# First-batch query parts of both attentions copied inside SBUF by two queues, in place of a store to DRAM and a load back

## What is computed

```python
q = (query @ Wq.T).reshape(B, q_len, H, dk).transpose(0, 2, 1, 3)
k = (key @ Wk.T).reshape(B, k_len, H, dk).transpose(0, 2, 1, 3)
v = (value @ Wv.T).reshape(B, k_len, H, dk).transpose(0, 2, 1, 3)
scores = jnp.einsum('bhqd,bhkd->bhqk', q, k) / jnp.sqrt(jnp.float32(dk))
attn = jax.nn.softmax(scores, axis=-1)
out = jnp.einsum('bhqk,bhkd->bhqd', attn, v)
x = x + out.transpose(0, 2, 1, 3).reshape(B, q_len, D) @ Wout.T + b_out
```

## Time and profile before

| | us |
|---|---|
| median of 3 runs | 1268.6 |
| profiled execution, first to last instruction | 1262.1 |
| PE busy in all | 1123.7 (89%) |
| attention 0, first to last matmul | 4.6 to about 226 |
| attention 1, first to last matmul | 470.3 to about 698 |

### The profile page before, as it was taken

How to read it: one execution, slowest core, us unless ns; L and a number is a source line. 1 busy time by engine, 2 the same in 40 slices (tenths; PEclk the granted TensorE clock), 3 DMA queues, 4 the chain that set the end, 5 groups by cost and what they waited for, 6 DMA issues and landing times. The chain is left out here.

```text
span 1262.1 us, 25941 instructions
## 1 busy us (share of the span) xinstructions
PE 1123.7 (89%) x8539; PEld 974.6 (77%) x8539; DVE 690.8 (55%) x1558; ACT 595.9 (47%) x1211; POOL 360.7 (29%) x502
## 2 busy tenths in 40 slices
PE   5999998739999984888998679999999999999997
PEld 4788786329888873555665379999999999999996
DVE  4755666652222226676767655555556555555556
ACT  3566666313222222776787334444445444444432
POOL 6566650112222205776630145000000000000261
PEclk8899999859999996999999879999999999999999
DMA  7774461548999957568471221223232232232132
GB/s 182 175 180 120 129 179 37 193 159 292 332 330 325 314 207 163 111 136 146 89 125 24 100 89 59 79 63 112 72 103 76 87 109 87 86 100 73 50 97 80
DMA packets 88137, 172.56 MB, mean 137 GB/s; under 512 B 11251, under 2 KB 59949, under 8 KB 81792
## 3 DMA queue, kind: packets, MB, share of 16 engines
q1 hardware_dynamic: 71712, 136.15, 39.0%
q0 software_dynamic: 9584, 29.32, 7.9%
q10 hardware_dynamic: 6768, 6.16, 1.4%
HBM read 133.11 MB, written 39.20 MB: 137 GB/s over the span
## 5 line engine op out<-in xcount | busy, mean ns | idle before, releaser
L2136 PE MATMUL e_ps<-xT_e,wp_e 128*128 128x384 f32 (+1 forms) x1344 | 245.2, 331 | 4.0 <-DVE wp_e L2010 4.0
L2136 PEld LDWEIGHTS e_ps<-xT_e,wp_e 128*128 128x128 f32 x1344 | 221.7, 188 | 5.4 <-issue 4.1
L639 DVE TENSOR_REDUCE att_ps<-att_ps 128x2 f32<-128x512 f32 (+1 forms) x224 | 155.3, 697 | 103.5 <-PE att_ps L986 63.2
L1968 ACT ACTIVATE act_a_e<-e_ps 128x256 f32<-128x256 f32 (+2 forms) x176 | 77.8, 442 | 159.9 <-PE e_ps L2136 150.9
L2066 DVE TENSOR_TENSOR hid_e<-act_a_e,e_ps 128x256 f32<-128x256 f32 (+2 forms) x176 | 87.0, 494 | 116.6 <-ACT act_a_e L1968 102.4
L892 ACT ACTIVATE probs<-att_ps 128x384 f32<-128x384 f32 (+1 forms) x256 | 130.4, 546 | 41.4 <-PE att_ps L1018 29.0
L1972 ACT ACTIVATE hidp_e<-hid_e 128x256 fp32r<-128x256 f32 (+2 forms) x176 | 83.8, 476 | 127.3 <-DVE hid_e L2066 121.5
L2153 PE MATMUL e_ps<-wp_e,hidp_e 128*128 128x256 f32 (+1 forms) x1008 | 138.4, 282 | 2.9 <-DVE xres L2026 1.2
L2068 DVE TENSOR_TENSOR hidp_e<-hid_e,hidp_e 128x256 fp32r<-128x256 f32 (+2 forms) x176 | 87.8, 499 | 95.5 <-ACT hidp_e L1972 90.1
L2153 PEld LDWEIGHTS e_ps<-wp_e,hidp_e 128*128 128x128 f32 (+1 forms) x1008 | 130.7, 183 | 4.9 <-issue 4.1
L1608 ACT ACTIVATE hid_e<-e_ps,b_ahead 128x128 f32<-128x128 f32 x188 | 53.7, 368 | 139.9 <-PE e_ps L1713 129.2
(11 more groups left out here) (235 smaller groups left out, 1850.0 us busy)
## 6 DMA issues: line engine op xcount, KB each, us to landing
w_e<-in_W SPq DMA_DIRECT2D x47, 1024.0 KB
w_e<-in_W SPq DMA_DIRECT2D x57, 384.0 KB, 3.1
ks<-parts SPq DMA_DIRECT2D x96, 128.0 KB, 4.7
qs<-parts SPq DMA_DIRECT2D x96, 128.0 KB, 5.2
parts<-cut SPq DMA_DIRECT2D x30, 384.0 KB, 3.2
x_e<-rows SPq DMA_DIRECT2D x8, 768.0 KB, 5.6
done<-y_e ACTq DMA_DIRECT2D x47, 128.0 KB
rows<-zeros POOLq DMA_DIRECT2D x8, 736.5 KB, 6.6
```

What stands on the lines that cost most here:

```text
L639: dve.tensor_reduce(tops_at(at[3])[:, qt, x0:x0 + heads], src, AX.X, ALU.max).then_inc(reduced, 1)
L1968: act.activation(act_a[:, u % 2, 0:n], ps[:, AB + u % 2, 0:n], ACT.Silu).then_inc(silu_ready, 1)
L2136: last = pe.matmul(ps[:, bank + u % 2, 0:n], weights(lot, c, pw)[:, (b * DC + d) * P:(b * DC + d + 1) * P], xT[:, px, d, t0:t0 + n], start ...
```

## The change

The queries of batch 0 no longer go through DRAM. `first_queries(eng, c)` is now a helper of the block: for each part, as it is cut, it issues one SBUF-to-SBUF DMA of 64 KB for each place of the part in the stack and for one chunk `c`. SP does chunk 0 (six DMAs), ACT chunk 1 (six DMAs); in attention 0 ACT does so before `take_values(0)`, in attention 1 before `square_root(1, ...)`. They count on `first_loaded[c]`, for which PE waits before the first score. The two counts that later waits rely on (`parts_stored[0]` and `stacks_loaded[0]`) SP now raises further down, before its loop over f.

```diff
-            def first_queries():
-
-                for part in range(PARTS):
-                    sp.wait_ge(piece_ready if part < PARTS - 1 else parts_ready[0], part + 1 if part < PARTS - 1 else 1)
-                    dst = parts_dram[0, 0, part].rearrange("c p s -> p c s")
-                    sp.dma_start(dst, parts[:, 0, KINDS.index(0), part]).then_inc(pieces_stored[part], 16)
-                for part in range(PARTS):
-                    sp.wait_ge(pieces_stored[part], 16)
-                    load_stack(sp, qs, 0, parts_dram, 0, 0, stacks_loaded[0], (part,))
-                sp.sem_inc(parts_stored[0], 16)
+        def first_queries(eng, c):
+
+            for part in range(PARTS):
+                eng.wait_ge(piece_ready if part < PARTS - 1 else parts_ready[0], part + 1 if part < PARTS - 1 else 1)
+                for r in range(len(STACK_Q)):
+                    if STACK_Q[r] == part:
+                        eng.dma_start(qs[r * DK:(r + 1) * DK, 0, c * HPC:(c + 1) * HPC], parts[:, 0, KINDS.index(0), part, c]).then_inc(first_loaded[c], 16)
...
             store_and_load(0, 0, 1)
-            first_queries()
+            first_queries(sp, 0)
...
             if causal:
                 load_flags(1)
+            for loaded in first_loaded:
+                sp.wait_ge(loaded, 16 * len(STACK_Q))
+            lead(sp, parts_stored[0], 16)
+            lead(sp, stacks_loaded[0], 16 * len(STACK_Q))
...
                 take_whole(f, f, 0)
+                if f == 0 and ye is not None:
+                    first_queries(act, 1)
                 if f == 0:
                     square_root(1, 1 if ye is not None else NORM - 1, 2)
+                if f == 0 and ye is None:
+                    first_queries(act, 1)
                 if ye is None:
                     take_values(f)
...
                 if g == 0 and u == 0:
-                    pe.wait_ge(stacks_loaded[j], 16 * len(STACK_Q) * 2 * (r + 1))
+                    if isinstance(n, int) and n == 0:
+                        pe.wait_ge(stacks_loaded[j], 16 * len(STACK_K))
+                        for loaded in first_loaded:
+                            pe.wait_ge(loaded, 16 * len(STACK_Q))
+                    else:
+                        pe.wait_ge(stacks_loaded[j], 16 * len(STACK_Q) * 2 * (r + 1))
```

More of the change, by code:

```diff
@@ L221, in attend_block @@
         wq_loaded, wk_loaded, wv_loaded = sem("wq_loaded"), sem("wk_loaded"), sem("wv_loaded")
-        v_cleared, piece_ready, pieces_stored = sem("v_cleared"), sem("piece_ready"), sems("pieces_stored", PARTS)
+        v_cleared, piece_ready, first_loaded = sem("v_cleared"), sem("piece_ready"), sems("first_loaded")
         x_loaded, ctx_loaded, flags_loaded = sems("x_loaded", 3), sems("ctx_loaded"), sems("flags_loaded")
```

## The result

The changed kernel takes 1275.1 us (median of 20 runs), the kernel before, in 20 runs beside it, 1268.87. The ratio is **1.0046, with a 95% interval of 1.0029 to 1.0064**: slower, by 0.0046 x 1268.87 = 5.8 us. Forecast were +4.05 us and 1272.7. A ratio in this text is the one on record with its interval; it is not the quotient of the two medians and can differ from it by about 0.001 (here 1275.1 / 1268.87 = 1.0049). One run of the kernel of experiment 12 took 2231 us, and is left out of its median and its ratio.

What follows compares the result with a forecast made beforehand. PE was taken as the bound, with no slack for batch 2's queries. Late batch 2 +2.85, clock +1.7 and attention 1 -0.5 gave +4.05 us on 1268.6: 1272.7 us, range 1266.0 to 1277.0.

Steps and rivals of the forecast that it cites:

- case A: The forecast itself: the late count decides at batch 2, +2.2 to +6.5 us, 1270.8 to 1275.1 us; chance 0.50.
- The landing of the copies: Start of attention 0: the last SBUF-to-SBUF query copy lands at 27.4 us, bounds 25.9 and 28.9.
- The first score: Attention 0, batch 0: first score at about 28.0 us, 2.7 us earlier, after ACT's values of batch 1 at 27.9.
- E: Start of attention 0: copies shorten nothing, PE waits for values at 27.9 or keys; alone 1268.6 us; chance 0.03.
- The count: SP raises parts_stored[0] only at 45.7 us, so POOL's cut of batch 2's keys starts then, not at 41.4.
- Batch 2: Attention 0: POOL's late root delays the query stack, landing at 79.4; batch 2 starts at 79.6, +2.85 us.
- PE's idle time and the clock: Ahead of batch 2 PE idles 6 us, then its granted clock falls to about half: +1.7 us.
- Attention 1: First score's wait goes and gathers may land sooner, late count harmless: -0.5 us, bounds -1.5 and +0.5.
- The 6.5 us outside the span: Whole kernel: the median of runs is 6.5 us above the profiled span; this difference was carried over unchanged.
- C: Count not late, SP's chain shrinks, batch 2 up to 3.2 us earlier: 1264.9 to 1268.4 us; chance 0.20.
- B: Count late, but clock holds while PE waits, or count costs only 1 us: +0.5 to +2.2; chance 0.17.
- D: Start of attention 0: slow copies with 512-byte rows, last landing at 34.9 us; +11.5 us, 1280; chance 0.10.

Runs made afterwards that it cites:

- experiment 12: Kernel before, queries still through DRAM, with POOL's root behind the cut of batch 2's queries and DVE's four copies moved ahead, in attention 0; 1266.26 us, ratio 0.9986.
- f3: Changed kernel without the late count, all twelve copies on SP, POOL's root behind batch 2's query cut, DVE's four copies moved ahead; 1270.02 us, ratio 1.0012.
- experiment 2: Changed kernel, but POOL's cuts of batch 2 wait for the landed copies and stored keys instead of SP's late count; 1267.54 us, ratio 0.9991.
- experiment 6: Changed kernel without the late count, with all twelve copies issued by SP and none by ACT; 1266.95 us, ratio 0.9971.
- e1: Kernel before, queries through DRAM, with only the count parts_stored[0] raised late, where the change raises it; 1276.29 us, ratio 1.0061.
- f2: Changed kernel with its late count, POOL's root behind batch 2's query cut and DVE's four copies moved ahead, in attention 0; 1271.42 us, ratio 1.0016.
- e4: Changed kernel with its late count, POOL's root moved behind the cut of batch 2's queries in attention 0; 1270.29 us, ratio 1.0018.
- e8: Kernel before, with four unused memsets on POOL between the root and the cut of batch 2's queries in attention 0; 1275.13 us, ratio 1.0037.
- e3: Changed kernel without the late count, POOL's root moved behind the cut of batch 2's queries in attention 0; 1271.28 us, ratio 1.0033.

## Why the prediction was right

The time, 1275.1, lies in the range (1266.0 to 1277.0), and the mechanism of case A happened: late count, late root, late queries of batch 2, idle PE, half clock. It is at the upper end of A (1270.8 to 1275.1), and its main term, +4.65, is beyond the bound of +4.35 that I gave it. By its own steps:

- **The landing of the copies: right.** The last of SP's is issued at 21.24 (21.84, the end of its row, less one issue) and lands 6.4 us later, at 27.64 (27.4 forecast, bounds 25.9 and 28.9). ACT's last lands at 26.3. The 18th to 19th us moves 138 GB/s at a share of 1.23, hardly more than the 131 of the earlier trace rows:

```profile
qs<-cut SPq DMA_DIRECT2D x1, 64.0 KB, 6.4
```

```profile
18.00:19.00 1.00, 0.00 (x0) 0.00 (x0) 1.00 (x4) 0.00 (x0) 0.00 (x0) 1.00 1.23 138
```

The Trainium skill's rule from "DMA: Bandwidth & Descriptors", that more queues save only issue time, agrees with the traces: the rate is nearly the same, and the last copy lands between 27.0 and 29.3 with two queues and at 28.3 and 28.6 with one (f3), on the clock of before. Its end, 28.9, lies in that spread, so after's 27.64 doesn't speak against it. Its sum, +5.55 us, is nearer to the 5.8 than mine, but by luck: the landing in after was not late, and the term was made longer by POOL and the loads.

- **The first score: mis-sized, 30.0 for 28.0.** I took 0.44 us for an issue, from the loads of the earlier trace rows. A copy takes 3.92 / 6 = 0.65 us on ACT, 4.04 / 6 = 0.67 on SP:

```profile
15.69 3.92 ACTq L362 DMA_DIRECT2D qs<-cut  x6
19.66 0.60 ACT L847 ACTIVATE vals<-att_ps 128x512 f32<-128x512 f32 x1 [4.79 <-issue]
...
29.22 0.60 ACT L847 ACTIVATE vals<-att_ps 128x512 f32<-128x512 f32 x1 [1.23 <-PE att_ps L972]
```

ACT starts the values at 19.66, not at 18.3, and ends those of batch 1 at 29.8, not at 27.9; 0.2 us later the first score comes. Of these 1.9 us the issues are 1.2: ACT starts on the rows of batch 1 at 20.63, 2.1 us later than before and not 0.9. The other 0.7 are PE's clock: it waits 4.18 us for `h` at 21.77 (1.67 before), and then works at 0.50 until 27.4 (before, until 25). The landing was on time, and ACT and PE decided: the gain at the start is 0.65 us, not 2.7, and other executions of the same code show none (31.54 in experiment 2). That is the mechanism of E, which I had at 0.03. The total doesn't feel it: batch 1 came 1.92 us earlier, since its queries landed 2.3 us earlier and PE ran batch 0 at a higher clock, and what PE had won it lost again ahead of batch 2. The step "with the 0.48 us of batch 1 won as well, PE stands before batch 2 at 73.5" was wrong: PE was ready at 81.37 - 5.85 = 75.5.

- **The count: right, 46.3 for 45.7.** The keys of batch 1 are stored and landed at 32.96, forecast at 32.95, and from there SP takes 46.23 - 32.96 = 13.3 us, forecast 12.8 from the same rows of before.

- **Batch 2: right in mechanism, +4.65 for +2.85.** Of the 1.8 us missing, 0.76 are the root's later start (51.71 for 50.95: the count's 0.6 and a little more on POOL). The root and the cut take 11.33 us where they took 10.77, +0.56. The loads end at 73.69 against 69.60, and land in 7.8 us for 7.4, +0.4. The forecast took POOL's chain behind the count as the same length as before; it was longer by each of these small sums.

```profile
qs<-parts SPq DMA_DIRECT2D x2, 128.0 KB, 7.8
```

- **PE's idle time and the clock: right.** 5.85 us for 6, though by two errors that cancel (batch 2 later than thought, PE ready later too). 1.8 us for 1.7. Batch 3 and all up to batch 6 stand 4.65 + 1.77 = 6.4 us behind; batch 7 stands 7.1 behind, as PE waits 1.30 us for its queries (0.62 before), and the last batch is 1.3 us shorter, which I did not follow. At the end of attention 0 it is 5.8.

- **Attention 1: -0.5 wasn't seen.** The first score comes 29.55 us after the stage's first matmul, 30.44 before, so 0.9 us were won as told (0.33 us of wait for 1.02). But POOL's cut for batch 2 starts 46.30 us after it, 46.46 before, and the stage is as long as it was. POOL keeps the pace; my sentence on that was right, and the half us that I took for sooner gathers had no ground in a row. SP's context load stands just before the cut, as in the earlier trace rows:

```profile
508.75 0.59 PE L994 MATMUL att_ps<-ks,qs 96*128 96x256 bf16 x2 [0.33 <-DMA qs<-cut]
```

```profile
524.52 0.42 SPq L421 DMA_DIRECT2D cst_ahead<-in_ctxT  x1
```

```profile
525.50 0.62 POOL L348 CAST cut<-full 128x512 bf16<-128x512 f32 x1
```

- **The 6.5 us outside the span: wrong.** The profiled execution of after ran 1272.02 us with a span of 1270.2, so 1.8 us lie outside. With the same 1.8, the profiled execution of before took some 1263.9 us, below all its 20 runs (1264.17 to 1275.69); that is the rest of the 6.5 us. The sum of terms wasn't touched by it, since I carried the difference over.

- **The rivals.** C (the count not late) was what experiment 2 made of the kernel, but its attention 0 is no shorter than before: its first score came 0.9 us later than before's, and PE reached batch 1 and 2 no earlier, without a wait for their loads. Its 1267.54 us don't show C's gain. B missed both its conditions, D its landing.

## What to carry to other kernels

When a wait is removed, look at every semaphore that the removed lines raised, who waits for it, and how far down the new place lies in that queue; here a count that moves no byte was worth 5.8 us, and asking for the landing itself in the waiting engine gave it back. Then look at the next batches, not only at the first: where their data land just when they are needed, an early start is worth little, and a delay is paid in full, with the clock on top. And before you put off a piece of work because nobody seems to wait for it, look at which instructions of the other engines it keeps company with.

## What the runs showed that I had not expected

- Issuing an SBUF-to-SBUF copy of 16x8x256 (64 KB) holds its queue for 0.65 us, more than the 0.45 us of a 128 KB load of 16x2x2048 and the 0.37 us of a 384 KB store. So it doesn't go with the bytes, nor with the number of contiguous pieces alone: by the shapes in the rows the copy has 128 of 512 bytes, the load 32 of 4 KB, and the store 768 of 512 bytes. What sets it was not varied by itself.
- On one queue the copies land soon after their issue: the twelve of experiment 6 took 7.74 us to issue and had a median of 4.6 us to landing, against 7.0 for SP's six and 6.8 for ACT's in after. They were issued later behind the same key loads; the last landed no later.
- DVE's four copies of 8x1024 bf16 take 1.44 us with POOL idle, 1.5 beside POOL's instructions of 128x10, 1.7 to 1.9 beside its copies of 128x256, 2.6 beside one `join_bias` of 128x512 (e1), 2.9 to 3.8 beside its cut of 128x512, 7.2 to 7.8 beside wide instructions without a pause. POOL was hardly slower (2.12 us for adding the masks either way, 2.86 for 2.50 of `join_bias`). The Trainium skill ("GPSIMD Engine Reference", Specifications) has the SBUF interfaces of the two engines shared, with contention for some DVE instructions; these runs agree, and show that DVE bears nearly all of it.
- PE fell to half its clock after or in idle times of 1.77 (f2, with another 0.46 close behind), 2.70 (e4) and 3.48 us (e8), not only after the nearly 6 us of the changed kernel; after 1.59 us (e3) it stayed at 1.00. It came back 3 us (e8) to 6 us (e4) after its work began again. From batch 2 to 3 that cost 1.3 us in e8, 1.8 in after and 2.3 in e1. Batch 0 of the kernel before, at 0.50 for its first 8 us behind 4.30 us of idle, keeps PE busy 1.6 us longer than that of the changed kernel.
